# A two-layer transformer-like block on one core: the order of the solve steps around a head, and one copy given to VectorE

## The reference

```
qkv = x @ W_qkv ; z = x @ W_z                       # 16 q, 16 k, 32 v heads of 128
qkv = silu(sum_j w[:, j] * shifted(qkv, 3 - j))     # causal convolution, 4 taps
q, k = l2norm(q), l2norm(k); beta = sigmoid(x @ W_b); decay = exp(-exp(A) * softplus(x @ W_a + dt))
for each t:                                         # state: 128 x 128 for each head
    state = state * decay_t
    state = state + k_t (x) ((v_t - k_t state) * beta_t)
    o_t   = q_t state
y = o * silu(z); y = y * rsqrt(mean(y*y) + 1e-6) * norm_w ; out = y @ W_out
```

## Time and profile before

| | |
|---|---|
| median of 3 runs | 1780.88 us (1780.53 to 1781.27) |
| the profiled execution | 1780.41 us, its span 1778.6 us |
| granted clock of PE, mean | 0.986 |
| PE busy | 1673.6 us (94%) |
| DVE busy | 1276.6 us (72%) |
| ACT busy | 1192.3 us (67%) |
| POOL busy | 1049.8 us (59%) |
| layer 1, one head (turn_v to turn_v, heads 2 to 14) | 69.6 us |

### The profile page before, as it was taken

The page is one execution under the profiler, slowest core; times in us unless marked ns, Lnnn a source line. Parts: engine busy times, 40 slices in busy tenths (PEclk is TensorE's granted clock), DMA queues, the critical chain, the costliest instruction groups (busy, mean ns, idle before and its releaser), DMA issues.

```text
span 1778.6 us, 35351 instructions
## 1 busy us (share of the span) xinstructions
PE 1673.6 (94%) x13560; PEld 1279.6 (72%) x13592; DVE 1276.6 (72%) x2248; ACT 1192.3 (67%) x2216; POOL 1049.8 (59%) x663
## 2 busy tenths in 40 slices
PE   7899999999998997999999999999999999999986
PEld 5676676767765675777787787877777877877775
DVE  7888888888876367967768667668677677686653
ACT  3335344353444466888888889888888788898872
POOL 2222312223124047989778888887887888788860
PEclk9999999999999998999999999999999999999998
DMA  3111110110103200110120101101101201111000
GB/s 139 35 38 65 34 68 34 50 52 34 68 1 106 77 19 1 37 61 25 37 60 26 37 30 56 37 25 38 59 26 37 60 26 37 40 46 37 8 1 25
DMA packets 51453, 75.24 MB, mean 42 GB/s; under 512 B 3392, under 2 KB 41792, under 8 KB 51312
## 3 DMA queue, kind: packets, MB, share of 16 engines
q1 hardware_dynamic: 51312, 73.28, 12.7%
HBM read 72.03 MB, written 1.25 MB: 41 GB/s over the span
## 4 chain that ended last, share of the span: by engine, by line
PE 51%; ACT 8%; DVE 7%; issue 3%; POOL 1%; DVEq 0%; POOLq 0%
PE bank L736 9%; PE bank L756 5%; PE bank L925 5%; PE bank L794 3%; PE bank L880 2%; PE bank L766 2%; DVE d_sil L1361 2%; DVE d_X L1407 2%; PE bank L807 2%; PE bank L817 2%; PE bank L888 2%; PE bank L901 2%; PE bank L864 2%; PE bank L902 2%; PE bank L903 2%
## 5 line engine op out<-in xcount | busy, mean ns | idle before, releaser
L1361 DVE SCALAR_TENSOR_TENSOR d_sil<-d_pre,d_w,d_sil 128x1024 f32<-128x1024 f32 x147 | 244.0, 1660 | 10.2 <-ACT d_pre L1113 9.9
L736 PE MATMUL bank<-xnT,d_w 128*128 128x512 f32 x480 | 242.3, 617 | 0.1
L189 PE MATMUL bank<-xnT,a_w 128*128 128x512 f32 x512 | 236.9, 596 | 0.0
L1686 POOL TENSOR_TENSOR d_dec<-d_dec,d_qk 128x384 f32<-128x384 f32 x128 | 134.9, 1083 | 172.2 <-ACT d_qk L1157 171.2
L489 POOL TENSOR_TENSOR a_hidc<-a_hid,a_comb 128x512 f32<-128x512 f32 x32 | 44.4, 1388 | 294.9 <-DVE a_hid L336 294.9
L1407 DVE CAST_PREDICATED d_X<-tables_sb,bank 128x512 bf16<-128x512 int32 x192 | 134.1, 699 | 77.8 <-PE bank L807 62.7
L1423 DVE TENSOR_TENSOR d_Rb<-d_V,bank 128x512 bf16<-128x512 f32 x128 | 87.6, 687 | 93.1 <-PE bank L880 92.7
L189 PEld LDWEIGHTS bank<-xnT,a_w 128*128 128x128 f32 x512 | 90.8, 192 | 78.5 <-issue 78.5
L481 POOL TENSOR_TENSOR a_qT<-a_rot_a,a_rot_b 128x512 f32<-128x512 f32 x64 | 81.3, 1271 | 100.7 <-DVE a_rot_b L325 100.7
L508 ACT ACTIVATE a_sg<-a_sm 128x384 f32<-128x384 f32 x64 | 33.0, 515 | 152.0 <-DVE a_sm L341 152.0
L1670 POOL TENSOR_SCALAR d_N<-d_pre,d_w 128x1024 f32<-128x1024 f32 x45 | 128.1, 2846 | 4.8 <-ACT d_pre L1113 1.9
(11 more groups left out here) (229 smaller groups left out, 4755.4 us busy)
## 6 DMA issues: line engine op xcount, KB each, us to landing
d_dec<-decay_scratch SPq DMA_DIRECT2D x32, 512.0 KB, 5.9
a_w<-w SPq DMA_DIRECT2D x16, 897.0 KB, 4.5
d_w<-w SPq DMA_DIRECT2D x16, 776.0 KB, 4.7
a_comb<-comb_scratch SPq DMA_DIRECT2D x16, 512.0 KB, 5.5
d_dec<-decay_scratch SPq DMA_DIRECT2D x32, 256.0 KB, 5.8
d_wo<-w SPq DMA_DIRECT2D x16, 256.0 KB, 3.0
f_w<-w SPq DMA_DIRECT2D x8, 256.0 KB, 4.7
x_sb<-x SPq DMA_DIRECT2D x2, 512.0 KB, 4.7
```

What stands on the lines that cost most here:

```text
L189: last = pe.matmul(psum[bank][:, :], wq(slot, part, k), xnT[:, k, half * HALF:(half + 1) * HALF], start=(k == 0), stop=(k == KT - 1))
L736: last = pe.matmul(psum[bank][:, :], cols(slot, (c * KT + k) * P, P), xnT[:, k, h * HALF:(h + 1) * HALF], start=(k == 0), stop=(k == KT - 1))
L1361: dve.scalar_tensor_tensor(sil[c][:, :, :], pre[c % 2][:, :, tap:tap + S], cols(slot, OC + 4 * c + tap, 1), sil[c][:, :, :], ALU.mult, ALU ...
L1686: pool.tensor_tensor(g, g, qk[b][:, :, :], ALU.mult).then_inc(s["p_done"], 1)
```

## The change

PE: at a = 2, `apply` issues its two products with `identb` before it waits for the right side. z(0, 1) goes from `between[2]` to `inner[1]`.

ACT: the first batch of decays goes from behind the second `first_w` to ahead of `round_r2`. In `conv_in` of input 0, its first half loses the plain copy for every head but the first, and its second half waits, before its own plain copy, until the first is counted.

DVE: `plain_in` makes that plain copy (128x512, from PSUM), last of `begin`. It waits for ACT's read of the same bank (`tapped`).

```
@@ PE apply
+                if a == 2:
+                    pe.wait_ge(s[f"dw_done{v}"], i * 2 + c + 1)
+                    for n, vec in enumerate((W0b, dWb)):
+                        pe.matmul(psum[4 + 2 * v][:, :], identb[:, :], vec[v][:, :, :].rearrange("p b d -> p (b d)"),
+                                  start=(n == 0), stop=False, skip_group_check=True)
                 if k == 0:
...
                     pe.wait_ge(s["r_done"], i * 10 + 2 * (3 * c + a - 1) + v + 1)
-                if a == 2:
-                    pe.wait_ge(s[f"dw_done{v}"], i * 2 + c + 1)
-                    for n, vec in enumerate((W0b, dWb)):
-                        pe.matmul(psum[4 + 2 * v][:, :], identb[:, :], vec[v][:, :, :].rearrange("p b d -> p (b d)"),
-                                  start=(n == 0), stop=False, skip_group_check=True)
@@ PE body
-                    between[1] = [z(0, 0)]
-                    between[2], inner[2], closing[2] = [z(0, 1)], [q(0, 0)], [q(0, 1)]
+                    between[1], inner[1] = [z(0, 0)], [z(0, 1)]
+                    inner[2], closing[2] = [q(0, 0)], [q(0, 1)]
@@ ACT conv_in
-                    act.activation(sil[c][:, 2 * h:2 * h + 2, :], ps, ACT.Copy, scale=cols(slot, OC + 4 * c + 3, 1))
+                    tap = act.activation(sil[c][:, 2 * h:2 * h + 2, :], ps, ACT.Copy, scale=cols(slot, OC + 4 * c + 3, 1))
+                    if c == 0 and h == 0:
+                        tap.then_inc(s["tapped"], 1)
+                    if c == 0 and h == 0 and i:
+                        continue
+                    if c == 0 and h == 1 and i:
+                        act.wait_ge(s["pre_done"], i * 8 + 1)
                     act.activation(pre[c % 2][:, 2 * h:2 * h + 2, 3:], ps, ACT.Copy).then_inc(s["pre_done"], 1)
@@ ACT body
                 update(i, 0)
+                if nxt:
+                    batch_decays(ni, ns, 0)
                 for v in range(2):
                     round_r2(i, v)
                 for v in range(2):
                     first_w(i, v, 1)
-                if nxt:
-                    batch_decays(ni, ns, 0)
                 change(i, 1)
@@ DVE conv, its first step
                         dve.wait_ge(s["pre_done"], i * 8 + 2 * c + 2)
+                        if c == 0:
+                            dve.wait_ge(s["tapped"], i + 1)
@@ DVE
+            def plain_in(i):
+                dve.wait_ge(s["tapped"], i + 1)
+                dve.wait_ge(s["conv_step"], i * 12)
+                dve.tensor_copy(pre[0][:, 0:2, 3:],
+                                psum[0][:, :].rearrange("p (b t) -> p b t", b=2)).then_inc(s["pre_done"], 1)
...
                     begin.append(lambda: columns(nj, ns, ni))
+                    begin.append(lambda: plain_in(ni))
```

More of the change, by code:

```diff
@@ L649, in layer1_phase @@
                  "conv_step sil_done kss_done krec_done n_done p_done plain_done tt1_done xp_done sz_done "
-                 "r_done wup_done0 wup_done1 dw_done0 dw_done1 mid_done nh_done nm_done nl_done tap_done y_done yss_done yssm_done acc_done col_done mask_done diag_done vb_done ysc_done").split()
+                 "r_done wup_done0 wup_done1 dw_done0 dw_done1 mid_done nh_done nm_done nl_done tap_done tapped y_done yss_done yssm_done acc_done col_done mask_done diag_done vb_done ysc_done").split()
         s = {n: m.sem(f"d_{n}") for n in names}
```

## The result

| | before | after |
|---|---|---|
| median | 1781.08 us (4 runs, 1780.53 to 1782.01) | 1770.32 us (4 runs, 1768.37 to 1771.01) |
| ratio | | 0.9937, 95% interval 0.9920 to 0.9955 |
| profiled execution, its span | 1780.41, 1778.6 us | 1768.37, 1766.5 us |
| one head, turn to turn (median of heads 2 to 14) | 69.56 us | 68.74 us |
| apply of step 0 to outputs, the solve | 21.69 us | 20.70 us |

A forecast was written before the change was run, and what follows sets the result against it. The prediction took PE to bound the kernel, with POOL close behind. It summed 6.8 us (heads 2 to 14), 0.3 (heads 0 and 1) and 0.5 (last head) to 7.6, giving 1773.3 us, range 1767.5 to 1779.5.

The forecast's parts named there:

- PE bounds the kernel, POOL comes next: PE, busy 94%, sets the time; POOL's convolution, through Silu of input 3 before `turn_v`, lies close behind.
- The decays: Exponentials moved ahead of `round_r2` on ACT: `apply` of step 3 loses 0.15 us, the 0.9 us `dWb` wait shrinks.
- the slower rival: Exp load stands behind the mask wait: 0.45 us longer in each of 15 heads, 1787.2 us; chance 11%.
- The solve: PE reaches `outputs` at 1405.93 instead of 1406.77, a gain of 0.84 us by the end of the solve.
- PE's edits: The `identb` pair runs in step 5's 0.28 us wait; moving z(0, 1) is worth 0 to 0.1, taken as 0.
- The last head: Without z or POOL work ahead, the `identb` pair fills a wait of about 0.25 in both chunks: 0.5 us.
- The plain copy: Moved from ACT to DVE: ACT's freed time becomes idle, DVE's copy is covered before `X`; gain 0.
- What POOL lets through: Silu of input 3 holds `turn_v`, so 0.52 us of PE's 0.84 comes through and 0.32 becomes a wait.
- Everything from the turn to the split is the same in both: PE's own path of 34.3 us is unchanged, so heads 2 to 14 each get 0.52 us shorter, 6.8 in all.
- Heads 0 and 1: POOL leaves little slack there; together they give 0.3 us, between 0.05 and 0.8.
- The rival "less": DVE's plain copy drags and `X` is 0.2 to 0.3 us late in 14 heads: 1776.1 to 1777.5; chance 14%.
- The rival "more": POOL's chain shortens, gaining 11.7 us (1769.2), or ACT's freed 0.48 helps the inversion (1767.1); chance 17%.

The follow-up runs named there:

- decays alone: The kernel before with only the first batch of decays moved ahead of `round_r2` on ACT; 1771.80 us, ratio 0.9943.
- PE's edits alone: The kernel before with only the `identb` products issued first and z(0, 1) moved between the residuals; 1771.31 us, ratio 0.9943.
- POOL shortened: Half of POOL's third tap product left out, not a usable kernel: 1778.02 us from the kernel before, 1764.45 us from the kernel after.
- the plain copy alone: The kernel before with only the plain copy moved from ACT to DVE; 1782.07 us, ratio 0.9999.
- Memsets on POOL: The kernel before with two small memsets added among POOL's decayed products, nothing else; 1778.57 us, ratio 0.9981.
- the last tap on DVE: The kernel after with the third tap of convolution 3 made by DVE instead of POOL; 1760.88 us, ratio 0.9879.

## Why the prediction was right, and where it was off

*PE bounds the kernel, POOL comes next.* Right. Shortening POOL gives before nothing in the solve or the turn, and gives after its wait in the turn back.

*The decays.* Right in kind: the load ran ahead of the wait for the masks, so the slower rival, the Exp load behind that wait, did not come. `apply` of step 3 stands 12.27 us behind the first `apply`, against 12.26 before. Its start is set by the rounding behind the exponentials, as worked out. I priced this at 0.15 lost, and that loss did not come: in decays alone `link` stands at 8.69, as before, and `apply` of step 3 at 12.27 too. The rounding starts 11.60 us behind the first `apply`, as worked out; with its 0.63 us it ends 0.04 before PE starts, where I had allowed more.

*The solve.* 0.84 forecast, 0.99 measured. The 0.15 is the loss at the rounding that did not come.

*PE's edits.* I put the pair of `identb` products into the sum as if it filled the 0.28 us wait of step 5. Alone it does. Beside the decays it does not: in before the two residuals of step 4 ran back to back behind the wait for ACT, and PE was through before DVE had made the right side of v = 0. With the decays moved, the second residual starts 1.04 us behind the first instead of 0.67, held by DVE's `dWb`, and DVE makes the right side meanwhile. Decays alone has no wait at line 861 in step 5 and shows the whole 0.98 (21.69 to 20.71). The sum was not harmed, the attribution was: the 0.28 came from the decays. z(0, 1) made `link` 0.13 us earlier (8.56 against 8.69), near the 0 to 0.1 that I gave; beside the decays `apply` of step 3 gained nothing by it.

*The last head.* 0.5 forecast for the pair, 16.74 to 16.22 us measured from its first `apply` to `outputs`. Decays alone shows 16.73 there, PE's edits alone 16.22.

*The plain copy.* 0 forecast, 0 measured, twice, and by the mechanism named: ACT waits for PE, DVE was idle.

*What POOL lets through.* This term was mis-sized. I allowed 0.15 us from the end of Silu to PE's first transposition, taken from a cast followed by narrow matmuls. It is 0.05. The slack was 0.63 and not 0.52, 0.11 for each of 13 heads: 1.4 us.

*Everything from the turn to the split is the same in both.* This is the step that failed. The stretch ahead of the solve, 41.59 us, fell to 41.41 in after, worth 0.18 a head, 2.3 us over 13. Its cause is not in the change's own instructions: two memsets on POOL do the same to before, POOL shortened does too, and the plain copy alone does nothing. The changed kernel turns PE and DVE earlier against POOL's chain, and with it the order of the pair shown under "Memsets on POOL" is the other one: DVE comes first. Head 11 of after:

```profile
1426.00 1.56 DVE L1369 SCALAR_TENSOR_TENSOR d_sil<-d_pre,d_w,d_sil 128x1024 f32<-128x1024 f32 x1
1426.46 2.01 POOL L1742 TENSOR_TENSOR d_Rb<-d_V,d_knorm 128x512 bf16<-128x512 f32 x1
```

A head can also fall the other way. Head 9 of the profiled execution of after took 69.40 us instead of 68.74. There DVE's first step had come 0.37 us later than in head 10 (20.65 against 20.28 us behind the turn of v = 0), for a reason that stays open; so POOL's operation came first and DVE's second step took 2.04 us again:

```profile
1288.31 1.04 POOL L1742 TENSOR_TENSOR d_Rb<-d_V,d_knorm 128x512 bf16<-128x512 f32 x1
...
1288.38 2.04 DVE L1369 SCALAR_TENSOR_TENSOR d_sil<-d_pre,d_w,d_sil 128x1024 f32<-128x1024 f32 x1
```

Together: 13 heads at 0.82 would be 10.7 us; with that one head, 904.24 - 894.24 = 10.0 measured over heads 2 to 14, against 6.8.

*Heads 0 and 1.* They gave 0.29, against 0.3, if they are taken from the turn of v = 0 to that of head 2 (147.37 and 147.08 us). That the figures agree is luck: the 0.3 was meant to reach the turn of v = 1, and head 2 of after waits for the Silu inside its turn, so from turn to turn of v = 1 the two heads gave nothing (147.37 and 147.42).

*The rival "less"* had the plain copy drag. It took 0.68 us. *The rival "more"* reached 11.7 us by way of a shorter POOL chain or a helpful ACT. The time came out near it, but by neither: POOL's chain is 33.47 us in both kernels.

## What to carry to other kernels

Before moving work off the chain that ends last, subtract from it the slack of the chain that ends just behind; here 0.63 of 0.99 us a head came through, and the rest came only when that second chain was shortened. When several waits follow one late engine, repair the first and look again before pricing the others. Between DVE and POOL look at who starts first where both work, since moving any engine's phase changes it, and filling POOL's idle time can cost more than it gives: here POOL's split came 1.7 us sooner, and the stretch ahead of the solve grew by 1.5 us.

## What the runs showed of the hardware

- A DVE operation with two SBUF inputs (128x1024, f32) takes 1.27 us when POOL rests and up to 2.96 us beside POOL's operations. In the pair under "Memsets on POOL" it took 2.04 us where POOL had started 0.08 us ahead of it, and 1.42 us where POOL started 0.31 us behind it.
- From the end of an ACT activation to a waiting PE it took 0.05 us behind Silu (to the f32 transpositions of the turn), 0.04 behind `round_r2` (1457.81 + 0.63 = 1458.44, `apply` at 1458.48) and 0.15 behind `dWb` (to line 880). `apply` and line 880 are both narrow bf16 matmuls, so their kind is not what makes the difference; what does is not shown.
- A table load had ended (1454.73 + 1.28 = 1456.01) 0.40 us before the wait of its activation did (1456.41), in ACT's idle time. It took 1.28 us, and nothing like a drain showed behind it: where no wait stood between, the activation followed within 0.02 us.
- Layer 0's identical code ended up to 4.6 us apart in the twelve profiled executions (637.22 to 641.79). The granted clock differed with it: 0.77 or 0.89 from 75 to 90 us, and from 525 to 555 us 0.89 in before and after and 0.77 in decays alone and in the last tap on DVE. Differences of 0.1% between two kernels needed the period of a head, not the time.
